# Second norm's scaling on ScalarE in two attention layers, and five convolution segments moved to the cross attention

## The reference, cut to what matters

```python
x = x + L0_xattn(layernorm(x), ctx, Wq, Wk, Wv, Wout, bout)     # 8 heads of 64, softmax(q k^T / 8) v, then Wout, + bout
x = x + L0_ffn(layernorm(x), router_w, w1, b1, w2, b2)          # 8 experts, each takes the 33 best tokens of a batch
x = x + L1_xattn(...)   # has a convolution whose taps K[d, 0:128] = 2 Re(sum_n dC exp(dtA l)) depend on the inputs alone
x = x + L1_ffn(layernorm(x), ...)                               # a small transformer of 2 layers, DEPTH = 2:

def layer(x):                                    # h8 heads of 64, window 64
    h = shift_token(x); q, k, v = split(h @ wqkv)
    q, k = rotary(l2norm(q) * qs, l2norm(k) * ks)
    x = x + local_attention(q, k, v) @ wo
    h = shift_token(x)                           # second 64 features come from the token before
    h = (h - mean(h)) / sqrt(var(h) + 1e-5) * lg + lb      # the second norm
    a, g = split(h @ w1 + b1)
    return x + (a * gelu(g)) @ w2 + b2
```

## Time and profile before

| what | us |
|---|---|
| median of 3 runs (1470.41 to 1477.22) | 1475.01 |
| profiled execution, its own time | 1466.48 |
| its span, first to last instruction | 1464.7 |
| first attention block | 0 to 87.24 |
| cross attention block | 87.24 to 157.21 |
| gathered mixture block | 157.21 to 241.51 |
| small transformer block | 544.24 to 813.65 |

### The profile page before, as it was taken

How to read it: one execution, slowest core, us unless ns; L and a number is a source line. 1 busy time by engine, 2 the same in 40 slices (tenths; PEclk the granted TensorE clock), 3 DMA queues, 4 the chain that set the end, 5 groups by cost and what they waited for, 6 DMA issues and landing times. The chain is left out here.

```text
span 1464.7 us, 25972 instructions
## 1 busy us (share of the span) xinstructions
PE 1263.5 (86%) x10478; PEld 932.0 (64%) x10478; DVE 738.9 (50%) x2181; ACT 519.7 (35%) x1160; POOL 408.3 (28%) x451
## 2 busy tenths in 40 slices
PE   6999487999877756887887799998989999987998
PEld 5868365788623433664666697795657774565776
DVE  5555663434489254874684315626832126756111
ACT  5534132443355322433343212213433324443332
POOL 7920692000333226754672400003000001040000
PEclk9999688999956678999998758999989989988999
DMA  4000401321290000000000000000021100000010
GB/s 136 1 4 2 186 1 66 94 67 50 105 233 1 1 31 1 1 1 0 1 1 1 9 2 2 1 4 2 1 82 41 43 14 1 1 3 29 30 44 30
DMA packets 46695, 48.42 MB, mean 33 GB/s; under 512 B 18960, under 2 KB 37904, under 8 KB 45552
## 3 DMA queue, kind: packets, MB, share of 16 engines
q1 hardware_dynamic: 46576, 46.76, 10.2%
HBM read 41.91 MB, written 4.85 MB: 32 GB/s over the span
## 5 line engine op out<-in xcount | busy, mean ns | idle before, releaser
L1027 PEld LDWEIGHTS bank<-scratch 128*128 128x128 f32 x1024 | 119.0, 192 | 13.9 <-issue 13.9
L1056 ACT ACTIVATE scratch<-bank 128x512 f32<-128x512 f32 x128 | 76.3, 597 | 135.1 <-PE bank L1017 135.1
L1075 DVE SCALAR_TENSOR_TENSOR x_res<-bank,scratch,x_res 128x128 f32<-128x128 f32 x128 | 36.0, 344 | 167.9 <-PE bank L1027 167.9
L1027 PE MATMUL bank<-scratch 128*128 128x128 f32 x1024 | 119.2, 275 | 0.0
L1017 PE MATMUL bank<-xnT,scratch 128*128 128x512 f32 x256 | 118.6, 608 | 0.0
L616 ACT ACTIVATE scratch<-bank 128x512 f32<-128x512 f32 x96 | 52.4, 594 | 89.3 <-PE bank L517 89.3
L575 DVE TENSOR_REDUCE scratch<-bank 128x4 f32<-128x512 f32 x96 | 63.1, 685 | 35.8 <-PE bank L2180 22.8
L1017 PEld LDWEIGHTS bank<-xnT,scratch 128*128 128x128 f32 x256 | 47.9, 197 | 49.0 <-issue 48.8
L440 POOL TENSOR_TENSOR ln_rstd<-ln_ve,ln_half 128x4 f32<-128x4 f32 x28 | 28.7, 1024 | 164.1 <-DVE ln_ve L419 164.0
L2428 POOL TENSOR_TENSOR scratch<-scratch 128x16 f32<-128x16 f32 x16 | 51.7, 3231 | 49.8 <-DVE scratch L2754 49.8
L581 DVE TENSOR_TENSOR scratch<-bank,scratch 128x512 f32<-128x512 f32 x96 | 61.4, 681 | 0.0
(11 more groups left out here) (526 smaller groups left out, 2886.4 us busy)
## 6 DMA issues: line engine op xcount, KB each, us to landing
scratch<-conv_kernels SPq DMA_DIRECT2D x8, 1024.0 KB, 11.1
scratch<-e_l_ffn_w SPq DMA_DIRECT2D x32, 256.0 KB, 2.9
scratch<-e_l_ffn_w SPq DMA_DIRECT2D x4, 1024.0 KB, 14.2
values<-scratch SPq DMA_DIRECT2D x8, 512.0 KB, 2.6
scratch<-values SPq DMA_DIRECT2D x8, 512.0 KB, 4.2
weights<-w_l_ffn SPq DMA_DIRECT2D x1, 3698.0 KB, 11.4
weights<-w_l_attn SPq DMA_DIRECT2D x1, 2560.5 KB, 8.9
weights<-w_l_attn SPq DMA_DIRECT2D x2, 1024.0 KB, 7.6
```

Of the source, the lines that this page charges most:

```text
L1027: mm = nc.tensor.matmul(ps[Y_BANKS[u % 3]][:, t * P:(t + 1) * P], hT[h][:, i, t * P:(t + 1) * P], wb[e % 2][:, i, :], start=(i == 0), stop ...
L1056: nc.scalar.activation(hT[u % 2][:, i, :], ps[UP_BANKS[i]][:, :], act_func) \
```

## The change

1. In the cross attention DVE adds y from its PSUM bank to `core.x` right away, after the subtraction of batch n+1's maxima. ACT's copy of y, the tile `y` and POOL's eight additions are gone. PE's wait for a bank that held y is now for DVE's addition. The second value projection of batch 0 is gone too.
2. Segments 2 to 6 of the taps run on POOL in the cross attention, behind the two bias additions. Segment 7 and tap 0 stay in the mixture, now behind a wait for the last of the gate-weighted one-hot matrices (`weighed.at(3)`).
3. In the small transformer `scale(g)` is two ACTIVATE instructions on ACT, Identity with `scale=rstd` and `bias=offset`. For that DVE's `measure` also writes `minus_mean` (128x1), and POOL's `root` multiplies it with rstd into `offset` (128x1). In a step ACT scales after the squares and ahead of the copied output. At a layer's end `scale(last - 2)` stands ahead of the table load for Gelu, `scale(last - 1)` after the second gelu, `scale(last)` after the eighth `take`.

```diff
@@ layer_l0_xattn
-        return fills + ([("v", n + 1)] if n + 1 < B else [])
+        return fills + ([("v", n + 1)] if 0 < n + 1 < B else [])
@@ POOL
-            for b in range(B):
-                pool.wait_ge(biased.sem, biased.at(b // (B // 2)))
-                pool.wait_ge(emptied.sem, emptied.at(place["y", b]))
-                xs = core.x[:, b, :]
-                nc.gpsimd.tensor_tensor(xs, xs, y[:, b % 2, :], ALU.add).then_inc(added.sem, added.up())
-            pool.wait_ge(added.sem, added.at(B - 1))
+            conv_kernels(core, pool, 1)
@@ PE, bank()
-                if f >= 2:
-                    pe.wait_ge(emptied.sem, emptied.at(f - 2))
+                if f >= 2 and order[f - 2][0] == "y":
+                    pe.wait_ge(added.sem, added.at(order[f - 2][1]))
+                elif f >= 2:
+                    pe.wait_ge(emptied.sem, emptied.at(emptied_at[order[f - 2]]))
@@ ACT
-                if 0 <= n - 2 < B:
-                    src = bank()
...
-                    nc.scalar.copy(y[:, n % 2, :], src[:, 0:D]).then_inc(emptied.sem, emptied.up())
@@ DVE, after the subtraction of batch n + 1
+                if 0 <= n - 2 < B:
+                    f = place["y", n - 2]
+                    dve.wait_ge(filled.sem, filled.at(f))
+                    dve.wait_ge(biased.sem, biased.at((n - 2) // (B // 2)))
+                    xs = core.x[:, n - 2, :]
+                    nc.vector.tensor_tensor(xs, xs, ps[F_BANKS[f % 2]][:, 0:D], ALU.add).then_inc(added.sem, added.up())
@@ layer_l0_ffn, POOL
-            conv_kernels(core, pool, 1)
+            pool.wait_ge(weighed.sem, weighed.at(3))
+            conv_kernels(core, pool, 2)
@@ conv_kernels
-    for a in range(2) if part == 0 else range(2, S):
+    for a in (range(0, 2), range(2, S - 1), range(S - 1, S))[part]:
@@ layer_l1_ffn, POOL root
-                pool.wait_ge(eps.sem, eps.at(g))
+                pool.wait_ge(eps.sem, eps.at(2 * g + 1))
+                if g > 0:
+                    pool.wait_ge(xn_made.sem, xn_made.at(2 * (g - 1) + 1))
                 nc.gpsimd.tensor_tensor(rstd, eps_var, power[:, 0:1], ALU.pow).then_inc(scaled.sem, scaled.up())
+                pool.wait_ge(scaled.sem, scaled.at(2 * g))
+                nc.gpsimd.tensor_tensor(offset, minus_mean, rstd, ALU.mult).then_inc(scaled.sem, scaled.up())
@@ ACT
+            def scale(g):
+                act.wait_ge(scaled.sem, scaled.at(2 * g + 1))
+                act.wait_ge(added.sem, added.at(g))
+                if g >= 2:
+                    act.wait_ge(handed.sem, handed.at(hand_at((g - 2) // 8, (g - 2) % 8 + 1)))
+                act.wait_ge(taken.sem, taken.at(hand_at(g // 8, g % 8)))
+                for part, src in ((0, res[:, g % 8, 0:HF]), (HF, moved[:, g % 2, :])):
+                    nc.scalar.activation(xn2[:, g % 2, part:part + HF], src, ACT.Identity, bias=offset, scale=rstd) \
+                        .then_inc(xn_made.sem, xn_made.up())
@@ DVE, measure, and scale is gone from there
+                nc.vector.tensor_scalar(minus_mean, mean_var[:, 0:1], -1.0, None, ALU.mult).then_inc(eps.sem, eps.up())
```

50 lines of the change are left out of this document (22 added, 28 removed).

## The result

| | before | after |
|---|---|---|
| median of the first comparison, us | 1475.67 (4 runs, 1470.41 to 1477.22) | 1440.53 (4 runs, 1439.21 to 1441.20) |
| ratio | | 0.9767, 95% interval 0.9741 to 0.9793 |
| profiled execution | 1466.48 | 1439.21 |
| all executions of the two kernels | 96, median 1473.0 (1464.2 to 1481.0) | 10, median 1441.2 (1435.7 to 1446.8) |

The kernel is 35 us faster by the first medians, 32 by all executions, 27 by the two profiled ones. So two things are to be explained: why the touched blocks gained more than 22, and why the three measures differ. The first question is one of terms; the second is about the executions.

A forecast was written before the change was run, and what follows sets the result against it. It took PE to bound the cross attention, DVE's chain stretched by POOL the mixture, and a DVE-POOL cycle the transformer. -12.4 + 2.2 - 11.8 = -22.0 us, from the median 1475.01, gave 1453.0, range 1443 to 1465.

The forecast's parts named there:

- the clock behind step 6: Small transformer: a shorter PE wait in step 6 saves slow-clock time, 1.0 us a layer, 2.0 in all, between 0 and 4.
- the mixture's scalings: Start of the mixture: DVE's eight 128x128 scalings shrink from 10.31 to 3.38 us without POOL's taps, 6.9 us saved.
- Mixture, 12.4 forecast: Mixture's routing: without most taps, DVE's eight scalings and two products shorten, saving 12.4 us, between 10 and 15.3.
- Cross attention, +2.2 forecast: Cross attention: taps hidden at no cost, y on DVE saves 0.5 and 0.6, new waits cost 3.3, together +2.2 us.
- three waits: Cross attention: in three turns PE's second fill behind y waits 1.1 us for y's bank, +3.3, between 1 and 4.
- the lock-out rival: Cross attention: DVE's operations with a PSUM operand wait for POOL's taps, 52 us, giving 1505; chance 0.04, weaker form 0.03.
- Transformer, steps 3 to 5: Small transformer: without DVE's scaling the cycle returns from 11.87 to 10.70 us, 3.5 us saved a layer, 7.0 for two.
- the stall was not passed on: Rival, small transformer: the cycle passes the stall on, half of 11.8 us is lost, giving 1460; chance 0.17 with outlasting taps.
- the pair on ACT is not the cycle's last: Rival, small transformer: ACT's queue becomes the cycle's last, 11.8 us saved becomes 4.3 lost, giving 1469.1; chance 0.02.
- Step 6 without the clock: Small transformer, step 6: without the scaling DVE starts its subtraction 2.0 us earlier, 4.0 us saved for two layers.
- Layer's end: Small transformer, end of a layer: scaling ahead of the table load costs +0.6 us a layer, +1.2 in all.
- The rival of 1447: Larger gain: gathering products at 2.4 GHz (2.9 us) and absorbed waits for y's bank (3.3) give 1447; chance 0.12.

The follow-up runs named there:

- the late taps: Kernel before with all six tap segments still in the mixture, begun only after the last one-hot matrices are made: ratio 1.0037.
- the filled step: Kernel before with 24 unused TensorE transposes in step 6 of each small-transformer layer, while it waits for VectorE: ratio 0.9989, block 267.07 us.
- three steps: Kernel after with ACT scaling only in steps 3 to 5 of a layer and DVE scaling the other five batches: 1453.4 us, ratio 0.9865.
- the steadied pair: Kernels before and after, each with five unused transposes in six steps at the end of the fourth attention: 1472.6 and 1445.8 us.
- part 3 alone: Kernel before with only the small transformer's scaling moved to ScalarE, cross attention and mixture unchanged: 1454.3 us, ratio 0.9867.
- parts 1 and 2: Kernel before with y on VectorE and five tap segments in the cross attention, small transformer unchanged: 1460.6 us, ratio 0.9903.

## Why the forecast was wrong, point by point

- **Which number failed.** 1440.5 lies 12.5 us below the forecast: 6.2 because the three blocks gained 28.2 instead of 22.0, 6.3 because the medians moved by more than the blocks. The step that failed among the terms is the clock behind step 6, 3.6 of the 6.2; the next is the mixture's scalings.
- **What bounds each block: right.** PE in the cross attention, DVE's stretched chain in the mixture, the DVE and POOL cycle in the transformer. All signs held, the order of the terms did not: the transformer gained most, 16.3, where the forecast had the mixture first.
- **Mixture, 12.4 forecast, 13.9 measured.** The mechanism is the one named, and the late taps show it by itself. The term mis-sized is the eight scalings: 10.31 to 3.38 was taken from rows 3, and they went to 2.36. The 3.38 was itself stretched: in the cross attention POOL adds the output bias to `core.x` while the last four run (1.26 us from 91.98 on in after, where DVE's eight take 3.38 again). A row from a place "without the taps" was not one without POOL. That is 1.0 of the 1.5 us. Another 0.4 is the first one-hot matrix, for which the forecast took nothing, since PE would be busy; but PE waits for the first one before its first gathering product. The gathering products stayed near the lower clock, as taken: 6.33 us at a mean of 0.60, for 5.84 at 0.65. The last segment beside the loop cost nothing.
- **Cross attention, +2.2 forecast, +2.0 measured.** All steps right: three waits of 0.98 for 1.1, the rest at -1.1, the taps hidden and over at 149, DVE's subtractions from PSUM at 681 ns. So the lock-out rival falls. The trace agrees with both halves of the rule on the shared port pair (the Trainium skill, SBUF — State Buffer, Who interferes with whom): 681 ns beside the taps, and for the scalings of SBUF operands 2.36 us without POOL's taps instead of 10.31 beside them.
- **Transformer, steps 3 to 5: 7.0 forecast, 7.35 measured.** 11.87 to 10.65 in six steps. Two of the rivals end here: the stall was not passed on, and the pair on ACT is not the cycle's last. The rule that add and multiply belong on VectorE (ScalarE: Activation LUTs, Rules for kernel authors, in the Trainium skill) would have made the edit 4.3 us slower; with 0.76 on ACT against 1.92 to 2.46 on DVE beside POOL, the trace goes against it at this place, and with 0.53 on an undisturbed DVE for it.
- **Step 6 without the clock: 4.0 forecast, 4.1 measured.** From `unite` to the subtraction it is 3.79 us instead of 5.85, and the filled step gives the same 2.07 for each layer.
- **The clock behind step 6 is the step that failed.** The forecast had 1.0 for a layer, 2.0 in all, between 0 and 4. It was 1.5 and 2.45 in step 6, and the second layer's down projection went from 4.57 to 2.94 us, 1.6 more: 5.6 in all. The 4.0 of step 6 are shown by the filled step. The 1.6 come with the change but not by way of step 6: the down projection kept its 4.57 where step 6 ran at 2.4 GHz (the filled step), and had 2.94 where step 6 came back at 1.2 GHz (three steps). It takes 4.55 to 4.58 in all eight traces with the scaling of steps 3 to 5 on DVE and 2.94 in all eight with it on ACT, while the first layer's is 4.57 in after too; how the clock there depends on those steps stays open. Rows 8 came from the first layer only, where the stretch at 1.2 GHz was short; in the second the same wait led to a longer one (1.97 and 2.69 for 1.71 and 2.04), which was in the trace and not read. The second layer's rows, of before and then of after:

```profile
772.05 1.97 PE L2507 MATMUL bank<-ident,scratch 128*128 128x128 f32 x8 [3.43 <-DVE scratch L2830]
776.05 2.69 PE L2541 MATMUL bank<-scratch 128*128 128x65 f32 x16
797.26 4.57 PE L2560 MATMUL bank<-weights,scratch 128*128 128x128 f32 x24 [2.41 <-DVE scratch L2783]
```

```profile
745.95 1.25 PE L2511 MATMUL bank<-ident,scratch 128*128 128x128 f32 x8 [1.39 <-DVE scratch L2842]
748.21 1.95 PE L2545 MATMUL bank<-scratch 128*128 128x65 f32 x16
768.89 2.94 PE L2564 MATMUL bank<-weights,scratch 128*128 128x128 f32 x24 [2.18 <-DVE scratch L2797]
```

- **Layer's end: +1.2 forecast, +0.45 measured.** From the first up projection to the down projection it is 9.95 us instead of 9.72, and 9.94 instead of 9.72 in the second layer.
- **From the sum to the time.** The forecast took the change from the median, since the blocks are the same. The profiled execution lay 6.5 us below the median of all executions of before; `layer_l2_xattn` ran wholly at 2.4 GHz in it and took 64.17 us, for 70 to 75 in the seven other traces with the scaling on DVE. With the right terms, 1475.0 - 28.2 = 1446.8, inside the range. (The rival of 1447 came to this number by two things that did not happen: PE at 2.4 GHz in the gathering products, and no waits for y's bank.) Of the remaining 6.3 us to 1440.5, 2.7 are what medians of three or four executions are off by, against 1473.0 and 1441.2 over all. The other 3.6 are the difference between 31.8 and 28.2; the steadied pair, with 26.8, speaks for chance, and no run settles it. The range allowed 3 us for medians, and the executions spread over 11 to 17.

## What to carry to other kernels

Take the price of an undisturbed instruction from a row where no other engine's instruction overlaps it, and check that in the timeline, not by what is said to be absent. Where an edit shortens a wait of TensorE, read the clock behind every instance of that wait, each layer's by itself: the time at the lower clock can be worth as much as the wait. Compare two kernels block by block, and only then by their medians: here the three touched blocks repeat to 0.5 us (once 1.4) where the whole varies by 10, and the block that varied most could be named from two traces of one program. Other untouched blocks varied too, if less often: one by 3.9 us (150.09 to 153.99), one by 5.5 (83.16 to 88.66, the low value once).

## What the runs showed of the hardware that was not expected

- TensorE ran the same first instructions of a block, behind the same wait of 0.72 us, at 2.4 GHz in one execution and at 1.2 GHz in another; the block took 64.2 to 75.0 us in sixteen traces.
- TensorE can be busy without a gap for 25 us and stay at 1.2 GHz: in the trace of part 3 alone that block has a granted clock of 1.00 over its first 12.5 us, then 0.52 over the next 25.0 us, in all of which TensorE is busy, and 1.00 again.
- GpSimd's product of 128x512 took 1.27 us with its table operand at one column, and 1.09 with it two columns (8 bytes) further, in all 64 of them (1.26 to 1.28, and 1.09 to 1.10), by that alone.
- The stretch at 1.2 GHz behind a wait is not a function of the wait: after 3.43 us it was shorter in the first layer than in the second (1.5 and 2.45 us lost; in the trace of parts 1 and 2 it was 1.5 in the second too), and after 2.91 us (with two columns added) longer than after 3.43. After 1.39 us, in steps 6 and 7 of after, the clock stayed at 2.4 GHz.
